# Attention of two layers: the weighted sums of a step in one block over all its queries, in place of two half blocks

## The reference, cut to what matters

```python
scores = jnp.einsum('bhqd,bhkd->bhqk', q, k)
scores = jnp.where(causal[None, None], scores, jnp.float32(-jnp.inf))
attn = jax.nn.softmax(scores, axis=-1)
out = jnp.einsum('bhqk,bhkd->bhqd', attn, v)
```

## Time and profile before

| | |
|---|---|
| Time, median of 3 runs | 1413.98 us (1411.87 to 1414.88) |
| The profiled execution's own time | 1409.36 us |
| Its span, first to last instruction | 1407.4 us |
| Mean granted TensorE clock | 0.907 |
| PE, DVE, ACT, POOL busy | 84%, 74%, 53%, 40% |

### The profile page before, as it was taken

How to read it: one execution, slowest core, us unless ns; L and a number is a source line. 1 busy time by engine, 2 the same in 40 slices (tenths; PEclk the granted TensorE clock), 3 DMA queues, 4 the chain that set the end, 5 groups by cost and what they waited for, 6 DMA issues and landing times. The chain is left out here.

```text
span 1407.4 us, 28130 instructions
## 1 busy us (share of the span) xinstructions
PE 1184.2 (84%) x8802; PEld 650.5 (46%) x8802; DVE 1041.5 (74%) x2108; ACT 740.0 (53%) x1137; POOL 566.7 (40%) x821
## 2 busy tenths in 40 slices
PE   0555666899989998999999767589999988999994
PEld 0333555234434443444443344335445436888872
DVE  5997997888868886888785255478778736677788
ACT  0552222056656665666567533136556666777772
POOL 5555222013322331223222155326557663456563
PEclk9987898599999999999999877569999998999996
DMA  3343870001221211121100013112222105577541
GB/s 98 97 124 94 126 92 0 16 4 56 93 81 41 75 62 55 47 69 62 40 2 3 1 57 95 39 35 64 51 61 57 50 23 196 159 237 236 188 120 60
DMA packets 98604, 107.92 MB, mean 77 GB/s; under 512 B 16225, under 2 KB 76454, under 8 KB 98480
## 3 DMA queue, kind: packets, MB, share of 16 engines
q1 hardware_dynamic: 93488, 97.83, 25.5%
q0 software_dynamic: 4992, 8.48, 1.8%
HBM read 64.67 MB, written 42.63 MB: 76 GB/s over the span
## 5 line engine op out<-in xcount | busy, mean ns | idle before, releaser
L1089 ACT ACTIVATE a_probs<-a_pst 128x1024 f32<-128x1024 f32 (+4 forms) x544 | 431.8, 813 | 248.6 <-PE a_pst L1003 245.9
L1111 DVE TENSOR_REDUCE a_tops<-a_ps 128x1 f32<-128x512 f32 (+9 forms) x624 | 363.0, 594 | 93.8 <-PE a_ps L987 78.2
L933 POOL TENSOR_SCALAR_AFFINE_SELECT a_probs<-a_probs 128x256 f32<-128x256 f32 (+3 forms) x384 | 182.3, 481 | 461.8 <-ACT a_probs L1089 460.0
L987 PE MATMUL a_ps<-kp,qp 96*128 96x512 bf16 (+9 forms) x1280 | 329.1, 313 | 8.6 <-issue 6.7
L1003 PE MATMUL a_pst<-qp,kp 99*128 99x512 bf16 (+4 forms) x1088 | 269.1, 335 | 3.2 <-ACT a_probs L1089 2.8
L1026 PE MATMUL a_po<-a_probs,vh 128*32 128x256 f32 (+2 forms) x3584 | 268.9, 373 | 2.5 <-POOL a_probs L933 1.5
L1111 DVE TENSOR_REDUCE a_tops_lead<-a_ps 128x1 f32<-128x512 f32 x256 | 173.0, 690 | 36.3 <-PE a_ps L987 32.8
L987 PEld LDWEIGHTS a_ps<-kp,qp 96*128 96x128 bf16 x1280 | 115.4, 103 | 101.5 <-DVE a_tops_lead L1111 34.8
L984 PE MATMUL a_ps<-mask_s,identb 128*128 128x128 bf16 (+8 forms) x624 | 148.5, 239 | 15.8 <-DVE a_tops L1111 7.1
L984 PEld LDWEIGHTS a_ps<-mask_s,identb 128*128 128x128 bf16 x624 | 60.9, 98 | 167.2 <-DVE a_tops L1111 77.7
L1644 POOL DMA_INDIRECT chosen_rows<-e_slot_y,e_slot_x x92 | 92.7, 1007 | 88.6 <-DVE e_slot_y L1832 66.6
(11 more groups left out here) (264 smaller groups left out, 1809.4 us busy)
## 6 DMA issues: line engine op xcount, KB each, us to landing
e_slot_w<-weight_parts SPq DMA_DIRECT2D x23, 1024.0 KB, 5.4
weight_parts<-a_cut SPq DMA_DIRECT2D x18, 512.0 KB, 3.9
k_parts<-o SPq DMA_DIRECT2D x48, 128.0 KB
qp<-q_parts SPq DMA_DIRECT2D x64, 96.0 KB
kp<-k_parts SPq DMA_DIRECT2D x32, 192.0 KB
slot_rows<-empty_row SPq DMA_DIRECT2D x4, 1495.0 KB, 27.0
e_slot_x<-slot_rows SPq DMA_DIRECT2D x23, 260.0 KB, 3.5
a_raw<-in_wraw SPq DMA_DIRECT2D x18, 256.0 KB, 4.3
```

Source lines behind the costliest of these rows:

```text
L933: pool.affine_select(out=seen, in_=seen, compare_op=ALU.is_ge, fill=0.0, base=m0, pattern=[[0, 2], [1, mw]], channel_multiplier=-1 if laye ...
L987: last = pe.matmul(bank[:, i * room:i * room + w], sb["qp"][slot][0:KROWS, j, f["qt"] * P:(f["qt"] + 1) * P], sb["kp"][slot][0:KROWS, j // ...
L1089: act.activation(probs[local % RING][0:st["rows"], 2 * part:2 * part + 2, st["off"]:CHUNK], p_st[part][0:st["rows"], :, st["off"]:CHUNK], ...
L1111: dve.tensor_reduce(out, scores, AX.X, ALU.max).then_inc(s["maxima_done"], 1)
```

## The change

A step is weighed in one block over all its query columns, whatever their number. Since only the first block of a step is put behind the first pair of the step two on, nothing stands behind the second pair any more. In steps that had two blocks, 8 matmuls of 256 (or 128 and 256) columns become 4 of 512 (or 384). The planner's clock for such a step gets shorter by 4 times 48, and with it every due time moves.

```diff
     def halves(self, st):
 
-        return [(st["off"], CHUNK)] if st["off"] >= CHUNK // 2 else [(st["off"], CHUNK // 2), (CHUNK // 2, CHUNK)]
+        return [(st["off"], CHUNK)]
```

## The result

| | before | changed |
|---|---|---|
| Median of 7 runs each | 1412.51 us | 1421.31 us |
| Ratio | | 1.0053 (95%: 1.0038 to 1.0067) |
| Span of the profiled execution | 1407.4 us | 1418.5 us |

By the ratio that is +7.5 us (5.4 to 9.5), and 8.8 between the two medians, where +17 was predicted: the sign held and, in layer 0, the size too; in layer 1 it did not. The two intervals do not overlap, so something moves between comparisons, and the loss is known only as 7 to 12 us.

A forecast was written before the change was run, and what follows sets the result against it. TensorE's stream was taken to set the pace in both layers, DVE behind it. Savings of 42 us against 59 of new waits gave +17, from a median of 1413.98 to 1431 us, range 1413 to 1444.

The forecast's parts named there:

- A block's fixed part: TensorE, both layers: each block carries 0.24 us independent of its columns; 176 merged steps save 42 us, 31 and 11.
- The round trip and the places in layer 0: At least 0.95 us from fill k's end to fill k+2's start; the new order adds 2.7 us of waits a unit.
- each of the five: Layer 0, TensorE waits ahead of fills 7, 11, 33, 34 and 37: 0.60, 0.34, 0.29, 0.55 and 0.24 us.
- scale_out's share: Layer 0, DVE: the reduction of fill 32 queues behind that of 31 and scale_out, so fill 34 waits 0.55 us.
- The other 0.7 us: Layer 0, per unit: fills 23, 24, 15 and 16 wait 0.26 us together; pairs and a block wait 0.44 for ScalarE.
- DVE's share falls: Layer 0: a sign that would show the forecast, DVE's busy share falling, not rising; no size given.
- The tail between them on DVE (1.35 us): Layer 1: with the tail between runs of fills, fills 0, 1 and 2 wait 1.0 us in all.
- +2.1 a batch: Layer 1: 5.0 us of new waits against 2.9 saved in a batch; +8 us over four batches.
- GpSimd costs nothing: GpSimd's queue: entries keep their order; masked probs are needed later than delivered, except at a batch's end, which was counted.
- Gain kept: Rival, chance 0.12: DVE's 17% in hand absorbs the runs of fills; 1372 us, or up to 1400 with half the waits.
- Cold clock: Rival, chance 0.08: PE runs short at batch ends and its clock falls, costing 10 us more: 1441.
- The 1413.98 and 1431: Whole kernel: the median before, 1413.98 us, and the median forecast after the change, 1431; forecast's chance 0.70.

The follow-up runs named there:

- e3: The changed kernel with scale_out of layer 0 due 400 columns earlier, ahead of fill 31 on VectorE: 1414.19 us, ratio 1.0053 to the kernel before.
- e7: The kernel before with GpSimd's selection of step 0 in layer 1 cut to 8 of 384 columns: 1400.42 us against 1410.26, ratio 0.9939.
- e8: The changed kernel with GpSimd's selection of step 0 in layer 1 cut to 8 columns: 1421.21 us, ratio 1.0083 to the kernel before.
- e6: The changed kernel with three quarters of each reduction left out: 1354.68 us, ratio 0.9625; 17.7 us faster than the kernel before with that cut.
- e11: The changed kernel measured once more, nothing altered, against the kernel before: 1418.72 us against 1407.09, ratio 1.0087.
- e4: The changed kernel with each block sorted in at 0.4 (layer 1: 0.35) of its length: 1403.86 us against 1407.79 for the kernel before, ratio 0.9965.
- e9: The changed kernel with blocks sorted in at 0.25 (layer 1: 0.4), fills due 1300 (1200) columns later: 1396.63 us against 1412.98 before, ratio 0.9881.

## Why the prediction was wrong, step by step

- **A block's fixed part, 0.24 us, and 42 us saved**: right. Blocks of 512 columns take 1.00 us for 0.99.
- **The round trip and the places in layer 0, 2.7 us of waits in a unit**: right, each of the five to 0.02 us, and scale_out's share by e3. The other 0.7 us, of ScalarE and of fills 23, 24, 15 and 16, are confirmed only as a sum, by the unit of 32.19. Layer 0 has +8.2 for +8. That DVE's share falls: right.
- **"The tail between them on DVE (1.35 us)" in layer 1**: this is the step that failed. The 1.35 us held 0.5 that belonged to the old order, a wait for GpSimd, and not to the operation. I used the duration of one row and had not asked why 32 elements took 0.70 us where L1125 on as many took 0.18. In the new order the tail takes 0.84 us, and fills 0, 1 and 2 wait 0.52 us for the 1.0 forecast. "+2.1 a batch" for layer 1 thereby missed what the new order gives back: 5.1 us at equal clock (e7). Layer 1 lost 1.3 us where +8 was forecast; of the 6.7 between them 5.1 are this, and some 2 are other waits of layer 1 that were counted too large (the ones listed add up to 4.7 a batch and not 5.0, and e8 has 6.0 for 8 at equal clock).
- **GpSimd costs nothing**: true of its queue, which is what the sentence looked at, and false of what its selection did to VectorE.
- **Gain kept** fell: DVE's 17% in hand were there, but at times when it had nothing to reduce. With a short round trip it comes in part (e6: 17.7 us of 42).
- **Cold clock**, with 0.08 the least of the rivals, did not decide the first comparison: at the three ends of layer 1 the granted clock was 0.86, 0.93 and 1.00 before and 1.00, 0.80 and 1.00 after, the same in sum. It cost about 1 us more in e11 (0.86, 0.93, 0.93) and 5.5 in e8 against e7. So it is a part of what moves between comparisons; how often it strikes was not measured.
- **The 1413.98 and 1431**: 1421 lies inside the range of 1413 to 1444, but the difference is 7.5 us (12 in the second comparison) for 17.

## What to carry to other kernels

Merging small blocks saves their fixed cost only where the producer that is squeezed out by the longer block doesn't arrive in a run afterwards: count how many of its pieces fall due inside the new block, and compare that with the buffers they rotate through. Measure the round trip of one buffer (here 0.95 us) and lay it over the new order piece by piece; that gave the five waits of layer 0 to 0.02 us. Before a duration is carried into another order, compare it with like operations nearby: one that is several times too long holds a wait, and the new order may drop it.

## What the runs showed that I had not expected

- A VectorE operation on 32 elements with two SBUF inputs takes 0.70 us in place of 0.19 when a GpSimd selection of 768 elements has started 0.19 us ahead of it. It shows as busy time, not as a wait. Without it in 11 places the kernel was 8.6 us faster, some 3 of them by a clock that held.
- A planner's rule, an entry that falls due inside a block goes behind it, was worth more than the change: sorting the same blocks in later (e4) took the changed kernel from 7 to 12 us above the kernel before to 4 to 5 below it, and later fills as well (e9) to 17 below.
- A lower granted clock at a batch's end makes a unit of layer 1 longer by about 1.1 us for each step from 1.00 to 0.93, 0.86 and 0.80 (means over 25 us), and it differs between runs of one kernel, so a difference of two or three us between two traces must be read with the clock beside it.
